# Layer 1's attention with TensorE's order of work for the steps of a group given by a table

## What is computed

```python
q = jnp.dot(x, Wq).reshape(b, t, H, HD).transpose(0, 2, 1, 3)          # 32 heads, HD = 16
kv = jnp.dot(x, Wkv).reshape(b, t, G, 2, HD).transpose(2, 3, 0, 1, 4)  # 8 groups
scores = jnp.einsum('bhqd,bhkd->bhqk', q, k)                           # 4 heads share k and v
scores = jnp.where(causal[None, None], -jnp.inf, scores)
weights = jax.nn.softmax(scores * (1.0 / HD ** 0.5), axis=-1)
ctx = jnp.einsum('bhqk,bhkd->bhqd', weights, v)
```

## Time and profile before

| | us |
|---|---|
| median of 3 runs | 1736.12 (1732.72 to 1740.18) |
| the profiled execution | 1737.15 |
| its span, first to last instruction | 1735.40 |
| the stage of this change | 1267 to 1540 in the span |

### The profile page before, as it was taken

How to read it: one execution, slowest core, us unless ns; L and a number is a source line. 1 busy time by engine, 2 the same in 40 slices (tenths; PEclk the granted TensorE clock), 3 DMA queues, 4 the chain that set the end, 5 groups by cost and what they waited for, 6 DMA issues and landing times. The chain is left out here.

```text
span 1735.4 us, 27207 instructions
## 1 busy us (share of the span) xinstructions
PE 1631.3 (94%) x8810; PEld 1220.1 (70%) x8810; DVE 1080.6 (62%) x2489; ACT 847.6 (49%) x1591; POOL 716.8 (41%) x740
## 2 busy tenths in 40 slices
PE   6899998999988999999999999899989999999998
PEld 5688887788776766776677777587755555568887
DVE  3556657999838767777777777435776776510222
ACT  3456555443326555555555555444245565653321
POOL 1212213444657656666556666376201111322221
PEclk9999999999999999999999999999989999999999
DMA  8522223221100000000000000373432332231111
GB/s 243 171 76 90 91 77 93 60 63 34 55 31 7 25 19 19 31 19 20 25 19 19 31 19 13 92 236 122 151 62 50 84 66 61 51 103 55 49 49 49
DMA packets 113020, 114.16 MB, mean 66 GB/s; under 512 B 39776, under 2 KB 72000, under 8 KB 112896
## 3 DMA queue, kind: packets, MB, share of 16 engines
q1 hardware_dynamic: 110592, 108.40, 21.9%
q10 hardware_dynamic: 2304, 4.20, 0.7%
HBM read 83.97 MB, written 28.44 MB: 65 GB/s over the span
## 5 line engine op out<-in xcount | busy, mean ns | idle before, releaser
L1463 ACT ACTIVATE a_p<-a_sm,a_nmax 128x640 f32<-128x640 f32 (+7 forms) x256 | 198.7, 778 | 142.6 <-DVE a_nmax L1424 140.9
L1506 POOL TENSOR_SCALAR a_p<-a_p,a_rinv 128x640 f32<-128x640 f32 (+7 forms) x256 | 191.9, 753 | 165.0 <-DVE a_rinv L1432 162.1
L1424 DVE CUSTOM_DVE_ANT_0 a_sm<-ps,maskb 128x640 f32<-128x640 f32 (+7 forms) x256 | 192.0, 750 | 98.4 <-PE ps L1368 96.5
L2360 DVE CUSTOM_DVE_ANT_0 ga_sm<-ps,strip 128x640 f32<-128x640 f32 (+1 forms) x224 | 163.1, 754 | 71.2 <-PE ps L2267 69.7
L2381 ACT ACTIVATE ga_pt<-ps 128x1024 f32<-128x1024 f32 (+1 forms) x192 | 147.9, 810 | 112.7 <-PE ps L2290 111.7
L1380 PE MATMUL ps<-ident,a_p 128*128 128x128 f32 x1152 | 172.4, 275 | 14.0 <-DVE a_pt L1439 13.8
L1380 PEld LDWEIGHTS ps<-ident,a_p 128*128 128x128 f32 x1152 | 135.3, 140 | 39.7 <-issue 16.9
L2421 POOL TENSOR_SCALAR_AFFINE_SELECT ga_pt<-ga_pt 128x512 f32<-128x512 f32 x64 | 40.7, 636 | 265.1 <-ACT ga_pt L2381 265.0
L1368 PE MATMUL ps<-kh,lq_qh 128*128 128x512 f32 (+4 forms) x384 | 128.8, 389 | 18.4 <-DVE a_nmax L1424 11.6
L940 DVE SCALAR_TENSOR_TENSOR idx<-ix_r,ix_sgc,idx 128x256 f32<-128x256 f32 (+6 forms) x105 | 90.7, 884 | 73.9 <-ACT ix_r L905 73.9
L1395 PE MATMUL ps<-a_pt,vst 128*64 128x512 f32 (+3 forms) x768 | 134.2, 492 | 1.9 <-DVE a_pt L1439 1.1
(11 more groups left out here) (313 smaller groups left out, 3979.2 us busy)
## 6 DMA issues: line engine op xcount, KB each, us to landing
idx<-ctx_d SPq DMA_DIRECT2D x32, 256.0 KB, 3.3
idx<-wvo_d SPq DMA_DIRECT2D x32, 256.0 KB, 3.8
ga_qst<-qkd SPq DMA_DIRECT2D x42, 128.0 KB, 4.2
f_wr<-in_L_ffn_w SPq DMA_DIRECT2D x18, 256.0 KB, 2.8
x<-in_L_attn_hidden_states SPq DMA_DIRECT2D x16, 256.0 KB, 4.3
op_wo<-in_L_attn_o_w SPq DMA_DIRECT2D x8, 512.0 KB, 5.0
ix_w<-in_L_attn_idx_wq_w SPq DMA_DIRECT2D x64, 64.0 KB, 1.9
ix_fo<-in_L_attn_o_w SPq DMA_DIRECT2D x8, 512.0 KB, 4.1
```

The lines of the kernel that those rows point to most:

```text
L1424: dve.tensor_tensor_reduce(out=in_row(sm[kind][:, 0:w], w), in0=in_banks(slots[kind], w), in1=in_row(maskb[:, MASK_OFF[t]:MASK_OFF[t + 1]] ...
L1463: act.activation(p[kind][:, v // 2 % 2, 0:w], sm[kind][:, 0:w], ACT.Exp, bias=nmax[:, v % 4:v % 4 + 1], scale=-1.0, accum_out=rsum[:, v % ...
L1506: pool.tensor_scalar(mine, mine, rinv[:, v % 4:v % 4 + 1], 1.0, ALU.mult, ALU.mult).then_inc(norm_done, 1)
L2360: dve.tensor_tensor_reduce(out=in_row(sm[kind][:, 0:w], w), in0=in_banks(slots[kind], w), in1=in_row(strip[:, S - w:], w), scale=-1.0, sca ...
```

## The change

The numbers in `SHARE` and the fixed pattern inside a step give way to a string for each step: k and K are the keys of part 0 and 1, u the next score unit, w the next weighing, t the transposition. The units are counted through all groups (four are ahead at a group's start, as before), and so are the weighings, which begin two behind. Step 2 holds two weighings and step 9 three (7, 8 and 9, the last of them of step 9 itself); steps 3, 10 and 11 hold none. So a weighing follows its step by two, one or none. In step 9 the transposition stands behind the weighing of step 8, and one score unit of the group after stands directly ahead of it. The waits on exponentials are the same; ScalarE's, VectorE's, GpSimd's and SP's order is unchanged.

```diff
-    LEAD = 3
+    LEAD = 4
+    TURN_AT = 9
...
-    SHARE = [4, 3, 2, 1, 4, 3, 4, 3, 4, 2, 1, 1]
+    ORDER = ("kuKuw", "kuKuw", "kuuwuKuwu", "kKu", "kuKuw", "kuKuwu", "kuKuwu", "kuuKwuu", "kKuwuu", "kwuuKuwutw", "kuKu",
+             "kuK")
...
-                lead = sum(SHARE[NSTEP - LEAD:])
-                for v in range(lead):
+                for v in range(LEAD):
                     score(1, v)
+                done, weighs = UNITS + LEAD, -LAG
                 for g in range(G1):
-                    done = lead
                     for s in range(NSTEP):
-                        later = g + 1 if s < NSTEP - LEAD else g + 2
-                        first = done if s < NSTEP - LEAD else done - UNITS
-                        units = range(first, first + SHARE[s]) if later < G1 else range(0)
-                        done += SHARE[s]
-                        keys(g, s, 0)
-                        one, two = (len(units) + 1) // 3, (len(units) + 1) // 3 + len(units) // 3
-                        for v in units[:one]:
-                            score(later, v)
-                        keys(g, s, 1)
-                        for v in units[one:two]:
-                            score(later, v)
-                        if s == NSTEP - LEAD and g + 1 < G1:
-                            turn(g + 1)
-                        if g * NSTEP + s >= LAG:
-                            weigh((g * NSTEP + s - LAG) // NSTEP, (g * NSTEP + s - LAG) % NSTEP)
-                        for v in units[two:]:
-                            score(later, v)
+                        for item in ORDER[s]:
+                            if item == "k":
+                                keys(g, s, 0)
+                            elif item == "K":
+                                keys(g, s, 1)
+                            elif item == "w":
+                                if weighs >= 0:
+                                    weigh(weighs // NSTEP, weighs % NSTEP)
+                                weighs += 1
+                            elif item == "t" and g + 1 < G1:
+                                turn(g + 1)
+                            elif item == "u":
+                                if done < G1 * UNITS:
+                                    score(done // UNITS, done % UNITS)
+                                done += 1
...
-                for s in range(NSTEP - LAG, NSTEP):
-                    weigh(G1 - 1, s)
+                for n in range(weighs, G1 * NSTEP):
+                    weigh(n // NSTEP, n % NSTEP)
```

More of the change, by code:

```diff
@@ L2274, in turn @@
                     if g > 0:
-                        pe.wait_ge(exp_done[0], START + (g - 1) * NSTEP + NSTEP - LEAD + 1)
+                        pe.wait_ge(exp_done[0], START + (g - 1) * NSTEP + TURN_AT + 1)
                     pe.transpose(ps[0:UNITS, 0, 0:P], nmax[:, g % 2], ident[:, :]).then_inc(turned, 1)
@@ L2286, in keys @@
                         pe.wait_ge(exp_done[p], START + g * NSTEP + s)
-                    if s == NSTEP - LEAD + 1 and g + 1 < G1 and p == 0:
+                    if s == TURN_AT + 1 and g + 1 < G1 and p == 0:
                         pe.wait_ge(nt_done, START + g + 2)
@@ L2399, in _ @@
                         exponential(g, s, 1)
-                        if s == NSTEP - LEAD and g + 1 < G1:
+                        if s == TURN_AT and g + 1 < G1:
                             take_shift(g + 1)
```

## The result

The changed kernel took 1745.58 us (median of 20 runs, 1739.31 to 1759.63) against 1736.93 before (median of 20, 1730.65 to 1741.73): a ratio of 1.006, 95% interval 1.0042 to 1.0077. The profiled execution has a span of 1741.9 us where before it was 1735.4. The forecast of 1728 was wrong, and its range of 1720 to 1737 did not hold the time.

A forecast was written before the change was run, and what follows sets the result against it. TensorE's stream was taken as the bound, standing still about 4 us of each 33.40 us group. Gains of 5 x 1.55 + 1.1 + 0.6 less 1.0 gave 8.5 us, from 1736.12 to 1727.6, stated as 1728; range 1720 to 1737.

The forecast's parts named there:

- Step 1, the stalls for VectorE: Inside a group: spreading the units removes TensorE's 3.60 us of stalls; new stalls add 0.8, bounds 0.5 and 2.0.
- the walk: Going through a group's new order with measured matmul spacings, counting smaller stalls once each: a period of 31.85 us.
- Step 2, two blocks ahead of the transposition: Ahead of the transposition: two 512-column weighing blocks add 1.98 us, making first keys to transposition 27.47.
- Step 3, the boundary: Transposition to next keys: 4.54 us, not 5.10, with TensorE idle some 1.3; period 31.85, gain 1.55 per steady group.
- The sum 5 x 1.55 + 1.1 + 0.6 - 1.0: Over the whole stage: gains of five steady groups, group 0 and group 6, less the last group's loss: 8.5 us.
- Rival (c): At group boundaries: the pause of some 1.3 us lowers TensorE's clock, giving 1737 or 1750; 13% for both forms.
- Step 4: First and last groups: group 0 gains 1.1 us, group 6 gains 0.6, group 7 loses 1.0 through waits.
- the slower form of (c): Behind each group boundary the clock stays low for 6.5 us, costing 3.3 each, 23 in all: 1750; chance 8%.

## Why the prediction was wrong, point by point

- **Step 1, the stalls for VectorE:** right. The stalls of the earlier trace rows are gone: from group 2's first keys to its transposition the changed kernel's trace has no wait for VectorE, and TensorE is idle for 0.21 of 27.64 us. The forecast for that distance was 27.47 by the sum and 27.3 by the walk.
- **Step 2, two blocks ahead of the transposition:** right in size, part of the same 27.64. It is also what made the pause, since they left the stretch in which they had covered the chain.
- **Step 3, the boundary:** the chain (4.51 against 4.54) and the pause (1.26 against "some 1.3") were right, and so was the observation on the earlier trace rows that the shifts landed just in time before: in the old order two DMAs fewer bought nothing, and two small ones more lengthened the period by 0.68. The steady period without a fall was 32.15 against the 31.85 that was taken (32.0 by the prediction's own sum), so a gain of 1.25 and not 1.55.
- **The step that failed is the price of that pause.** The sum 5 x 1.55 + 1.1 + 0.6 - 1.0 charged its length and put the clock at nothing. Rival (c) named the mechanism and its place, but gave it 13% and, from the earlier trace rows, 3 or 6.5 us at half clock, 1.5 or 3.3 us each. In the trace it was 10 us and 4.1 us each, at three of the six boundaries ahead of groups 1 to 6, and 3 us more in the last group and again behind it. The recovery in the earlier trace rows stood in other work, and this stage's was longer. The nearer rows were at the stage's own start in the trace of before, ahead of the first of the earlier trace rows:

```profile
1266.64 0.28 PE L2093 MATMUL ps<-ident,ga_nmax 128*32 128x128 f32 x1 [1.12 <-DVE ga_nmax L1979]
...
1268.00:1284.00 16.00, 14.13 (x40) 8.90 (x40) 8.81 (x24) 4.87 (x6) 1.91 (x3) 0.50 0.44 76
```

  The clock went low 0.7 us behind a wait of 1.12 and stayed low for 17 us, with score units and then this stage's own mix of work. I had read that as the start of a stage and not as a price.
- **The Trainium skill's rule** ("TensorE: Matmul & The Clock Gate", section "What's actually happening": the lower rate is the default, recent activity releases it) pointed at this pause. The traces agree with it in direction: falls came behind the pauses wherever these were put (10 us at half clock behind 1.26 in the changed kernel, 17 behind 1.12 ahead of a transposition), and filling the pause to 0.17 ended them in the trace. But a fall did not follow every such pause, and the sentence gives no price.
- **Step 4:** group 6 gained 0.38 against 0.6, and group 0 2.04 against 1.1, which was partly luck: its clock was low for 14 us and not 17 in this execution. The last group's waits were 0.76 and 0.18 against 0.8 and 0.2. What I missed is the end of the stage, where GpSimd's scaling is the last thing and TensorE's pause ahead of the next stage grew by 0.6 us, with another fall behind it. With the clock's part of the last group, 3.5 us were lost there and not 1.0.
- **The range** left out the slower form of (c) on its 8%. With two pauses of known size on either side (1.11 held, 1.84 fell), a forecast of 1.3 and the fall behind 1.12 at this stage's start, nothing in the trace bounded that chance so low. The time of 1745.58 lies near the 1750 of that slower form, and partly by luck: the prediction had a smaller price at all seven boundaries, the trace a larger one at three.

## What to carry to other kernels

When a change gathers TensorE's scattered stalls into one pause, look in the trace of before for the shortest pause behind which the granted clock fell (1.12 us here), and for how long it stayed low in this kind of work, and not only at the time that the pause costs. A longer pause after which it held elsewhere is no assurance: here it held behind 1.47 ahead of the next stage. A handful of stalls that the profile shows with 0.15 to 0.96 us were cheaper here than one of 1.26. If a chain of transposition, copy and DMAs has to be waited for, leave it work to run beside, by starting it earlier, by running the producer further ahead, or by fewer DMAs. A few matmuls that compute nothing are a quick test for a clock cause, and in this kernel they took back what the change had lost. If the record has the mean granted clock of every run, compare versions at an equal clock as well.

## What the runs showed of the hardware

This is from one kept trace of each of eleven versions. In the middle of the stage, pauses of TensorE of up to 0.97 us left it at 2.4 GHz. Of the 22 between 1.05 and 1.28 us, 14 had a fall to 1.2 GHz behind them and 8 had none, some with the same work around them. Of those of 1.46 and more it fell around five (1.46, 1.74, 1.79, 2.68, 2.86) and held behind one, of 1.55. Ahead of the next stage, whose matmuls are 128x128x512, it held behind all seven pauses of 1.47 to 1.53 and fell behind three of four of 2.09 and 2.10. At the stage's start it fell in all eleven traces, at most 2.6 us behind a wait of 1.12 that has shorter ones beside it. So these figures are no threshold.

Once low, it stayed low for 3 to 17 us in the middle of the stage and for 14 to 27 at its start, although in the middle of the stage TensorE was busy for 88% or more of every such stretch, and for all of most. The kernel before, too, had one run of 56 with a mean clock of 0.977 (1746.47 us), as low as the changed kernel's in its trace, so the pauses that held in one trace need not hold in each execution. Why the same pause falls at one boundary and not at the next, and why the way back differs so much, was not tested and stays open.

Small DMAs of SP from the same rows to DRAM took 0.28 to 0.29 us each to issue and lengthened the chain by about 0.33 each (from the transposition to the next keys 5.10 us without, 5.74 with two, 6.42 with four). A shift DMA within the core takes 0.64 to issue with eight rows and 0.59 with sixteen.
